# Attention over 16 batches on one core: half of the heads prepared earlier, and a new order on VectorE

## The reference, cut to what matters

```python
# L0_cond: x (16, 128, 256), mask (16, 256)
xt = transpose(x, (0, 2, 1))
q = xt @ Wq.T                                   # 8 heads of 16
scores = scale * einsum('bhqd,bhkd->bhqk', qh, qh)
logits = (scores * cmask + (1 - cmask) * NEG) * rmask
attn = softmax(logits, axis=-1)
ctx = einsum('bhqk,bhkd->bhqd', attn, qh)
out = transpose(ctx @ Wo.T, (0, 2, 1))
# L0_ffn: w = lut[idx], 16 values, for gate, up and down
h = silu(gate(out)) * up(out);  x = x + down(h)
# then the second block: RMS norm, 16-head attention, 4 experts, top 1
```

## Time and profile before

| | |
|---|---|
| profiled execution | 782.84 us, span 781.2 us |
| median of 3 runs | 780.7 us (778.14 to 783.45) |
| TensorE matmul | 605.0 us busy, 77% |
| TensorE weight load | 375.2 us, 48% |
| VectorE | 430.9 us, 55% |
| ScalarE | 322.0 us, 41% |
| GpSimd | 111.8 us, 14% |

### The profile page before, as it was taken

The page is one execution under the profiler, slowest core; times in us unless marked ns, Lnnn a source line. Parts: engine busy times, 40 slices in busy tenths (PEclk is TensorE's granted clock), DMA queues, the critical chain, the costliest instruction groups (busy, mean ns, idle before and its releaser), DMA issues. The chain is left out here.

```text
span 781.2 us, 15202 instructions
## 1 busy us (share of the span) xinstructions
PE 605.0 (77%) x4891; PEld 375.2 (48%) x4923; DVE 430.9 (55%) x957; ACT 322.0 (41%) x575; POOL 111.8 (14%) x145
## 2 busy tenths in 40 slices
PE   1456788867778869999956787788628999999992
PEld 1134455544455445555533454454414666666662
DVE  2455665675665664334336999999852333333331
ACT  1133454544454543233336777777502222222220
POOL 3401111111111001000000000000011333333321
PEclk9576666786666798999989999999958999999997
DMA  8863333333333320000036566555210111111110
GB/s 281 180 166 79 75 88 96 93 93 76 75 90 87 87 73 2 1 1 0 0 76 179 126 147 146 145 147 137 75 21 28 42 41 40 38 40 43 44 34 3
DMA packets 32739, 62.42 MB, mean 80 GB/s; under 512 B 7109, under 2 KB 19975, under 8 KB 30280
## 3 DMA queue, kind: packets, MB, share of 16 engines
q1 hardware_dynamic: 22112, 23.99, 10.7%
q0 software_dynamic: 6432, 18.46, 10.5%
q10 hardware_dynamic: 4168, 19.61, 9.7%
HBM read 58.81 MB, written 7.82 MB: 85 GB/s over the span
## 5 line engine op out<-in xcount | busy, mean ns | idle before, releaser
L1178 DVE TENSOR_REDUCE nmax<-PB 128x2 f32<-128x512 f32 x128 | 83.7, 677 | 93.8 <-PE PB L780 93.8
L536 ACT ACTIVATE probs<-PC 128x512 f32<-128x512 f32 x128 | 69.5, 595 | 132.2 <-PE PC L792 132.1
L780 PE MATMUL PB<-small 64*128 64x256 bf16 x256 | 46.6, 377 | 69.2 <-DMA small<-small 69.2
L1562 DVE TENSOR_TENSOR probs<-PC,probs 128x1024 bf16<-128x1024 f32 x19 | 23.3, 1225 | 79.9 <-ACT probs L729 65.6
L729 ACT CAST probs<-PC 128x1024 bf16<-128x1024 f32 x19 | 19.2, 1012 | 113.7 <-PE PC L1090 95.6
L764 PE MATMUL PA<-small,wq 128*128 128x256 f32 x128 | 50.6, 534 | 13.9 <-DVE identb L1142 13.9
L1082 PE MATMUL PA<-arena,probs 128*128 x227 | 54.2, 390 | 7.7 <-issue 3.9
L780 PEld LDWEIGHTS PB<-small 64*128 64x128 bf16 x256 | 12.8, 104 | 92.0 <-issue 70.6
L1101 PE MATMUL PD<-arena,probs 128*128 x456 | 53.0, 273 | 2.5 <-issue 2.5
L1082 PE MATMUL PB<-arena,probs 128*128 x210 | 48.6, 379 | 0.9
L1101 PEld LDWEIGHTS PD<-arena,probs 128*128 128x128 bf16 x456 | 44.3, 98 | 8.3 <-issue 3.2
(11 more groups left out here) (188 smaller groups left out, 1175.5 us busy)
## 6 DMA issues: line engine op xcount, KB each, us to landing
arena<-idx_low ACTq DMA_DIRECT2D x15, 1024.0 KB
wst<-in_w_all SPq DMA_DIRECT2D x48, 256.0 KB, 2.8
arena<-in_w_all POOLq DMA_DIRECT2D x16, 384.0 KB, 6.3
arena<-in_idx_all ACTq DMA_DIRECT2D x1, 2176.0 KB, 11.4
arena<-in_cond SPq DMA_DIRECT2D x16, 128.0 KB, 3.3
small<-in_x SPq DMA_DIRECT2D x16, 128.0 KB, 2.1
small<-small SPq DMA_DIRECT2D x64, 32.0 KB
arena<-idx_low POOLq DMA_DIRECT2D x2, 1024.0 KB, 15.2
```

Of the source, the lines that this page charges most:

```text
L536: nc.scalar.activation(probs[:, c, o], PC[:, o], ACT.Exp, scale=SCALE0).then_inc(S["ex"], 1)
L780: ins = mm(PB[:, s * 512 + qt * T:s * 512 + (qt + 1) * T], qs[r, par, c * T + qt * P:c * T + (qt + 1) * P], ks[r, par, c * T:(c + 1) * T], ...
L1178: v.tensor_reduce(nmax[:, c, s, :], PB[:, s * 512:(s + 1) * 512].rearrange("p (a k) -> p a k", k=T), AX.X, ALU.max, negate=True).then_inc( ...
L1562: v.tensor_tensor(hT_lo, PC[:], hT_hi, ALU.subtract).then_inc(S["hTl"], 1)
```

## The change

Four engines get another order in the pass; no instruction is added or removed but that the look-up is issued in two halves.

- TensorE: projection 0 stands between the two s of chunk 0, projection 1 in chunk 1, projections 2 and 3 behind the two s of chunk 3. The look-up's first half stands behind chunk 1, its second between the two s of chunk 2, with outputs0 behind chunk 2.
- ScalarE: the first half of the stacks stands behind the second pair of exponentials and waits only for the transposed scores that read this half; looked_up and the load behind it stand after the third pair, context_out after the fourth, the second half of the stacks at the end.
- VectorE: lows of half 0 stands behind the fifth maximum, lows of half 1 behind the maxima; then add_max, then one_hot.
- SyncE and GpSimd have the same lists, with other times for what they wait for.

```diff
@@ -517,7 +517,7 @@
                 o = slice(h * 512, (h + 1) * 512)
                 act.wait_ge(S["pq"], 2 * b + h + 1)
                 if not (isinstance(b, int) and b < 2):
-                    act.wait_ge(S["st"], 8 * (b - 1))
+                    act.wait_ge(S["st"], 8 * (b - 2) + 4 + 4 * h)
                 nc.scalar.activation(ks[:, par, o], PA[:, o], ACT.Identity, bias=cst[:, C_EV:C_EV + 1]).then_inc(S["ka"], 1)
                 nc.scalar.copy(qs[:, par, o], PA[:, o]).then_inc(S["qa"], 1)
 
@@ -558,14 +558,15 @@
                 exps(i - 1, 0)
                 values(i - 1, 1 - par)
                 exps(i - 1, 1)
+                if after:
+                    stacks(i + 1, 1 - par, 0)
+                exps(i - 1, 2)
                 looked_up(i - 1)
                 load_hot(i + 1, 1 - par)
-                exps(i - 1, 2)
+                exps(i - 1, 3)
                 if before:
                     context_out(i - 2)
-                exps(i - 1, 3)
                 if after:
-                    stacks(i + 1, 1 - par, 0)
                     stacks(i + 1, 1 - par, 1)
 
             body(1, 1, before=False)
@@ -806,16 +807,18 @@
                 if s == 1:
                     ins.then_inc(S["ctx"], 1)
 
-            def look_up(c, par):
-                pe.wait_ge(S["onehot"], c + 1)
-                pe.wait_ge(S["q2"], min(c + 1, B) if isinstance(c, int) else c + 1)
-                if isinstance(c, int) and c >= B:
-                    pe.wait_ge(S["c"], LAST)
+            def look_up(c, par, part_=None):
+                if part_ != 1:
+                    pe.wait_ge(S["onehot"], c + 1)
+                    pe.wait_ge(S["q2"], min(c + 1, B) if isinstance(c, int) else c + 1)
+                    if isinstance(c, int) and c >= B:
+                        pe.wait_ge(S["c"], LAST)
                 bank = PD[:, 512:1024].rearrange("p (h c) -> p h c", h=2)
-                for j in range(LPC):
+                for j in range(*{None: (0, LPC), 0: (0, LPC // 2), 1: (LPC // 2, LPC)}[part_]):
                     ins = mm(bank[:, :, j * LG:(j + 1) * LG], hot[:, par, j * P:(j + 1) * P],
                              lutw[:].rearrange("p h g -> p (h g)"), start=True, stop=True)
-                ins.then_inc(S["lmm"], 1)
+                if part_ != 0:
+                    ins.then_inc(S["lmm"], 1)
 
             def max_rows(b):
                 pe.wait_ge(S["mc"], 3 * b + 3)
@@ -850,15 +853,18 @@
                     for s in range(2):
                         scores(i, par, c, s)
                         scores_T(i - 1, 1 - par, c, s)
-                    if c == 0:
-                        project_v(i - 1, 1 - par, half)
-                    if c == 1:
-                        look_up(i - 1, 1 - par)
-                    if c == 2 and before:
-                        outputs0(i - 2)
-                    if c >= 2 and after:
-                        project(i + 1, 1 - par, 2 * c - 4)
-                        project(i + 1, 1 - par, 2 * c - 3)
+                        if after and c in (0, 1) and s == 0:
+                            project(i + 1, 1 - par, c)
+                        if (c, s) == (0, 1):
+                            project_v(i - 1, 1 - par, half)
+                        if (c, s) == (1, 1):
+                            look_up(i - 1, 1 - par, 0)
+                        if (c, s) == (2, 0):
+                            look_up(i - 1, 1 - par, 1)
+                        if (c, s) == (2, 1) and before:
+                            outputs0(i - 2)
+                        if after and c == 3:
+                            project(i + 1, 1 - par, 2 + s)
                 contexts(i - 1, 1 - par, 0)
                 max_rows(i)
                 contexts(i - 1, 1 - par, 1)
@@ -1169,7 +1175,7 @@
                 o = slice(h * 512, (h + 1) * 512)
                 v.tensor_tensor(low[:, o], PA[:, o], qs[:, par, o], ALU.subtract).then_inc(S["lo"], 1)
 
-            def maxima(b, before=False):
+            def maxima(b, before=False, low_at=None):
                 for c in range(4):
                     for s in range(2):
                         dve.wait_ge(S["sa"], 8 * b + 2 * c + s + 1)
@@ -1179,6 +1185,8 @@
                                         AX.X, ALU.max, negate=True).then_inc(S["max"], 1)
                         if before and 2 * c + s < 3:
                             normalise(b - 2, 2 * c + s + 1)
+                        if low_at is not None and (c, s) == (2, 0):
+                            lows(b + 1, low_at, 0)
                 dve.wait_ge(S["max"], 8 * b + 8)
                 unless_first(dve, S["mt"], b)
                 cols = mcol.rearrange("p q r (s m) -> p r s q m", s=2)
@@ -1215,13 +1223,11 @@
             def body(i, par, half, before=True, after=True):
                 if before:
                     normalise(i - 2, 0)
-                maxima(i, before)
-                if after:
-                    lows(i + 1, 1 - par, 0)
-                one_hot(i, par, half)
-                add_max(i, par)
+                maxima(i, before, 1 - par if after else None)
                 if after:
                     lows(i + 1, 1 - par, 1)
+                add_max(i, par)
+                one_hot(i, par, half)
 
             dve.wait_ge(S["kprep"], 1)
             lows(0, 0, 0)
```

## The result

The changed kernel takes 807.0 us (median of 4 runs, 798.6 to 811.4) against 780.2 us before (median of 4 runs). The prediction had 758, with 736 to 783 as its range.

What follows compares the result with a forecast made beforehand. Bound: TensorE's 3.8 us wait per pass for low-part copies, with low clock after it. Passes of 14.9 us (13.5 + 1.4) instead of 16.68 save 24.9 us over 14, less 1.9: 23 us, so 758 us, range 736 to 783.

Steps and rivals of the forecast that it cites:

- The wait for the copies: TensorE's scores waiting for low-part copies, 3.8 us in each of 14 waits: gone or under 0.5 us.
- Z: Zero of the prediction's walk through a pass, in us: the start of the transposes of the maxima.
- a late copy as a rival: Second half's copies 1.5 us later, or one-hot caught by GpSimd: 0.6 to 0.7 us more per pass, 767 us; chance 0.08.
- The pass at the full clock: Head-stage loop pass walked at the full clock: 13.5 us instead of 16.68, 44.5 us less over 14 passes.
- The wait of outputs0 for looked_up: New TensorE pause before outputs0, until ScalarE's looked_up frees the bank: about 1.9 us per pass.
- The clock: TensorE's granted clock low for 5 us per pass, each costing 0.27 us: 1.4 us more, 14.9 us per pass.
- TensorE's 1.0 us for separated groups: Score groups of a chunk no longer side by side: 0.25 x 4 = 1.0 us more per pass on TensorE.
- The last look-up: Hot-row load issued 1.9 us later; one_hot(16) and the last batch's contexts wait: 1.9 us more, once.
- GpSimd and VectorE's turn: At the pass's turn GpSimd's multiplications catch VectorE's one-hot: 0.15 us per pass, 2 us in all; bound 0.73 per pass.
- The sum: Loop pass 14.9 us instead of 16.68, 24.9 us less over 14 passes, less 1.9: 23 us gained.
- The slower rival: Separated score groups at a clock that never rises: 18.5 us per pass, 27 us more, 808 us; chance 0.11.
- the prediction's own signs of being wrong: In the changed trace: outputs0 doesn't wait, the fifth score group waits for a DMA, or passes stay above 16.5 us.

Runs made afterwards that it cites:

- e1: Kernel before, with each in-loop load of look-up rows cut from 1 MB to 64 KB: 726.1 us.
- e4: Changed kernel, with the 1 MB load issued by SyncE behind both patches instead of by ScalarE: 780.9 us.
- e2: Changed kernel, with each in-loop load of look-up rows cut from 1 MB to 64 KB: 778.7 us.
- e7: e4 with six idle matmuls ahead of outputs0, where TensorE waits for looked_up: 748.8 us.
- e11: e10 with the two score groups of each chunk side by side again, projections behind the second group: 746.8 us.
- e10: e4 with the look-up issued whole behind chunk 1 and looked_up right behind the second pair of exponentials, no idle matmuls: 747.5 us.
- e6: Changed kernel, with VectorE's order at the turn as before (one-hot, sum, second low part): 801.9 us.
- e12: Kernel before (no split of the heads), with SyncE's load, VectorE's new turn and eight idle matmuls behind the second contexts: 743.1 us.

## Why the prediction was wrong

- **The wait for the copies: wrong, and this is the step that failed.** "With the 3.64 us of today they land at Z+13.3 ... the wait disappears." The 3.64 us were read as the copies' own time. e1 shows 1.3 us without the load; the scores before start 11.5 to 12.7 us after the load's issue. The change moves the first half's copies from 7.2 to 7.9 us behind that issue to beside it, and in nine of 14 passes to 0.2 us behind it. In place of no wait stand six of 1.0 to 4.3 us and low passes after them: 26 us by e4, 28 by e2. The prediction had both pieces: it says under its rivals that today's copies "already meet the tail of that load", and by its walk the load is issued at about Z+8.8, beside the copies at Z+8.5 to Z+9.6. It asked for neither what part of the 3.64 us the tail is, nor what the load does to the copies there. It had a late copy as a rival, but for the second half, and at 1.5 us; the fifth score group never waits in the changed kernel.
- **What the copies' wait was worth: wrong by the same step.** With the load out of the way the old order takes 12.4 us per pass (e1), 4.3 less than before, and the new one 15.9 (e2). The change was to win 3.2 us per pass at the full clock by going around a wait that was mostly the load's.
- **The pass at the full clock: right.** 13.5 us walked, 13.5 in e2, 13.4 in e4 and e7. The wait of outputs0 for looked_up: right in kind and place, 1.25 us instead of 1.9; TensorE came to it 0.5 us later than walked and looked_up ended 0.3 us sooner (e2).
- **The clock: right in kind, too small in both factors.** I took 5 us per pass at the low level and 0.27 us for each. With no late copy the granted clock is 0.80 over 15.9 us (e2) or 0.78 over 15.8 (e4), 6.4 to 7.0 us at the low level, and 17.2 against 13.5 us for 10.3 us makes 0.36 each. So 2.4 us per pass instead of 1.4, 14 us in all. The 0.27 came from a pass of 18.5 us at the low level throughout, with TensorE busy 17.3; the window from 205.44 to 226.16, low but for its last 1.2 us, has TensorE busy 19.5 and lasts 20.7. Rows that the prediction summed as low were partly at the full clock, which rose within the 1.80 us for two projections (217.62) and within the 3.02 us for 32 contexts (295.42); the 0.62 us of the transposes are at the full clock. At the low level one projection takes 1.22, sixteen contexts 1.94 and the transposes 0.95:

```profile
206.40 1.22 PE L765 MATMUL PA<-small,wq 128*128 128x256 f32 x2
...
222.40 1.94 PE L805 MATMUL PD<-probs,vu 128*32 128x256 f32 x16
224.27 0.95 PE L831 MATMUL PD<-identb,small 128*128 128x128 bf16 x8
```

- **TensorE's 1.0 us for separated groups:** not on the path (e11). As TensorE's own time it stands: full-clock passes have 11.4 us of matmuls in e10 and 10.2 in e11.
- **The last look-up: wrong.** Its one-hot no longer waits for the load, so the 1.9 us forecast for it weren't paid. The stretch behind the loop is 6.2 us longer all the same, with outputs0's wait and a clock at the low level where it was up before (sixteen contexts take 1.94 us, where they took 1.07):

```profile
308.17 1.94 PE L805 MATMUL PD<-probs,vu 128*32 128x256 f32 x16 [1.31 <-ACT probs L536]
```

- **GpSimd and VectorE's turn:** e6 shows no difference of the turn. In the changed kernel every one-hot takes its usual 1.28 or 1.29 us, so the 0.15 us per pass weren't paid. In e7 the two do meet, in both orders. A multiplication behind a one-hot takes 1.67 us where it was 0.73, and a one-hot behind a multiplication 1.71 where it was 1.28:

```profile
154.91 0.73 POOL L407 TENSOR_TENSOR small<-arena 128x256 f32<-128x256 f32 x1 [0.54 <-DMA arena<-in_cond]
155.01 1.71 DVE L1181 TENSOR_SCALAR arena<-arena,cst 128x4096 bf16<-128x4096 bf16 x1
...
209.51 1.28 DVE L1181 TENSOR_SCALAR arena<-arena,cst 128x4096 bf16<-128x4096 bf16 x1
209.71 1.67 POOL L407 TENSOR_TENSOR small<-arena 128x256 f32<-128x256 f32 x1 [0.83 <-DMA arena<-in_cond]
```

The Trainium skill's rule (SBUF — State Buffer, "Who interferes with whom") that such a tensor_scalar and a GpSimd instruction exclude each other is borne out by these rows. No run shows it on the path.

- **The sum:** measured pass 18.0 = 13.5 (walked) + 2.4 (clock without late copies) + 2.1 (load, 18.0 - 15.9). The prediction had 13.5 + 1.4 + 0. The 18.0 is from the profiled execution; at the median of the runs, 4.4 us lower, the last term would be 1.8. The slower rival gives nearly the measured time, 808, by luck: it has a clock that never rises at 18.5 us per pass, and the clock was 0.72. Of the prediction's own signs of being wrong one came, passes above 16.5 us; outputs0 did wait, and the fifth score group didn't.

## What to carry to other kernels

When a small transfer looks slow, set its landing against the issue of every large transfer, not only against its own: a landing that keeps its distance from the large one's issue, and not from its own, belongs to that one. Before work is moved in time, list what the DMA queues carry at the new moment; a large load goes behind the small urgent copies, best in their own queue. A wait that a load causes is cheaper to remove at the load than by moving the work around it: e12 keeps the old order of the heads and is the fastest with the full load, though it has idle matmuls as well. And a gain that removes a wait of TensorE is sure only if no new pause takes its place, since a short one can cost the clock of the following pass.

## What the runs showed of the hardware that I had not expected

- Copies of 32 KB issued by SyncE 0.2 us after ScalarE's issue of a 1 MB load could be used only 10.6 to 11.0 us after the load's issue (six waits), though they are in another queue. At each of the six the DMA share falls with the start of the scores, from 0.14 to 0.37 in the microsecond before to 0.02 to 0.08 in the one after. With the load cut to 64 KB (e2) and the same order of issues, no scores waited. Issued 0.6 to 0.75 us ahead of the load, they weren't waited for.
- With a pause of 1.25 us per pass the granted clock was 0.70 in two passes of three (e2, e4), and 1.6 us of idle matmuls in its place brought it to 1.00 (e7). Yet e1 has a pause of 1.54 us and keeps 0.94. So the length of the pause alone isn't what decides; what stands around it differs (look-up halves and separated score groups in e2), and which of these it is stays open.
